# Attention in double steps with shift groups of two pairs, a reordered beginning, and later turns of the feed-forward inputs

## The reference

```
x = x + attention(layernorm(x))     # 16 heads of 64; q, k, v, softmax over 256, heads (with swapped axes) @ Wp + bp
x = x + ffn(layernorm(x))           # layernorm with gain and bias, w1 (512 x 128) and w2 (128 x 512) rounded to
                                    # -1, 0, 1 by their mean size, exact gelu, a second layernorm over 512
```

## Time and profile before

| what | value |
|---|---|
| median of 3 runs | 992.97 us (990.68 to 994.6) |
| profiled execution, its own time | 992.29 us |
| its span, first to last instruction | 990.5 us |
| granted TensorE clock, mean of the core | 1.000 |
| busy share PE / DVE / ACT / POOL | 98 / 86 / 74 / 87% |

### The profile page before, as it was taken

How to read it: one execution, slowest core, us unless ns; L and a number is a source line. 1 busy time by engine, 2 the same in 40 slices (tenths; PEclk the granted TensorE clock), 3 DMA queues, 4 the chain that set the end, 5 groups by cost and what they waited for, 6 DMA issues and landing times.

```text
span 990.5 us, 39211 instructions
## 1 busy us (share of the span) xinstructions
PE 968.2 (98%) x15932; PEld 767.8 (78%) x15932; DVE 854.4 (86%) x1743; ACT 733.4 (74%) x1180; POOL 861.8 (87%) x849
## 2 busy tenths in 40 slices
PE   7899999999999999999999999999999999989998
PEld 6577777787787887777778878877888887767776
DVE  6898988888888898899888988898888988768787
ACT  4687777778777777777777777777777778677775
POOL 5789898989886999999999999999899999878885
PEclk9999999999999999999999999999999999999999
DMA  6112232342323333223333332233433333367885
GB/s 136 44 31 53 47 74 53 62 64 64 79 43 51 64 84 65 61 51 59 85 63 64 58 83 39 61 61 83 65 63 64 63 64 63 79 126 158 168 171 129
DMA packets 242786, 74.08 MB, mean 75 GB/s; under 512 B 218032, under 2 KB 240304, under 8 KB 242608
## 3 DMA queue, kind: packets, MB, share of 16 engines
q1 hardware_dynamic: 240528, 71.05, 36.7%
q10 hardware_dynamic: 2080, 0.52, 0.3%
HBM read 11.41 MB, written 8.39 MB: 20 GB/s over the span
## 4 chain that ended last, share of the span: by engine, by line
PE 92%; DVE 2%; ACT 2%; issue 1%; DMA 1%; POOL 1%; SPq 0%; DVEq 0%; ACTq 0%; POOLq 0%
PE S L765 11%; PE PV L790 8%; PE M L725 7%; PE PV L792 6%; PE PV L791 6%; PE QK L712 5%; PE QK L714 5%; PE QK L713 5%; PE misc L765 5%; PE S L757 5%; PE M L843 2%; PE M L808 2%; PE M L845 2%; PE M L844 2%; PE misc L757 2%; PE M L810 2%
## 5 line engine op out<-in xcount | busy, mean ns | idle before, releaser
L1325 POOL TENSOR_TENSOR pl<-p 128x1024 f16<-128x1024 f32 x253 | 476.6, 1896 | 33.1 <-ACT p L1102 32.8
L1526 DVE TENSOR_REDUCE negmax<-M 128x4 f32<-128x1024 f32 x252 | 306.7, 1217 | 22.2 <-PE M L725 16.2
L1110 ACT ACTIVATE QKh<-QK 128x512 f16<-128x512 f32 x251 | 149.5, 596 | 142.2 <-PE QK L714 141.4
L1102 ACT ACTIVATE p<-S,s_exp 128x1024 f32<-128x1024 f32 x173 | 192.2, 1111 | 56.9 <-PE S L765 56.3
L790 PEld LDWEIGHTS PV<-V,p 128*128 128x128 bf16 x2048 | 186.6, 98 | 47.1 <-issue 36.3
L790 PE MATMUL PV<-V,p 128*128 128x65 f16 x2048 | 214.8, 193 | 4.5 <-DVE O L1540 3.6
L791 PE MATMUL PV<-V,p 128*128 128x64 f16 x2048 | 213.2, 192 | 0.0
L792 PE MATMUL PV<-V,pl 128*128 128x65 f16 x2048 | 212.5, 194 | 0.0
L1546 DVE TENSOR_TENSOR QKl<-QK,QKh 128x512 f16<-128x512 f32 x251 | 172.3, 687 | 43.3 <-ACT QKh L1110 42.2
L791 PEld LDWEIGHTS PV<-V,p 128*128 128x128 bf16 x2048 | 189.0, 97 | 4.7
L792 PEld LDWEIGHTS PV<-V,pl 128*128 128x128 f16 x2048 | 188.7, 97 | 0.0
(11 more groups left out here) (246 smaller groups left out, 2472.4 us busy)
## 6 DMA issues: line engine op xcount, KB each, us to landing
y_kept<-yTb SPq DMA_DIRECT2D x32, 128.0 KB, 1.7
yT<-y_kept SPq DMA_DIRECT2D x16, 256.0 KB, 3.4
result<-X SPq DMA_DIRECT2D x15, 256.0 KB, 3.0
X<-in_L_attn_query SPq DMA_DIRECT2D x7, 512.0 KB, 4.2
OT<-O SPq DMA_TRANSPOSE x64, 4.1
shift<-negmax SPq DMA_TRANSPOSE x63, 2.3
O<-in_L_attn_Wk ACTq DMA_DIRECT2D x2, 256.0 KB, 4.8
O<-in_L_attn_Wq SPq DMA_DIRECT2D x2, 256.0 KB, 5.6
```

The lines of the kernel that those rows point to most:

```text
L1102: e.activation(p32[r][:, :, :, :].rearrange("p i m n -> p (i m n)"), score_bank(p)[:, :], ACT.Exp, scale=s_exp[:, :]).then_inc(s_ex, 1)
L1325: e.tensor_tensor(pl[r][:, :, :, :].rearrange("p i m n -> p (i m n)"), p32[r][:, :, :, :].rearrange("p i m n -> p (i m n)"), p_high(r).rea ...
L1526: e.tensor_reduce(dst[:, :, NB * jj:NB * jj + NB], max_bank(p)[:, :].rearrange("p (i t m) -> p i t m", i=2, t=NB), AX.X, ALU.max, negate=T ...
```

## The change

It does eight things:

1. GP is 2 instead of 4: 128 shift groups instead of 64. Q_LEAD goes from 7 to 5, MAX_LEAD from 6 to 4. `shift_in` becomes two semaphores, one for each buffer.
2. Ahead of step 0 stand now pairs 0 to 3 of queries and keys and 0 to 2 of maxima. On ACT, the part up to step 0's end is written out in a new order; Wv's scaling comes ahead of the first shift, Wvh behind exps(0).
3. The statistics of batch 2 go from step 0 to 4, its norm, split and bias follow later too. The maxima of Wp and g2 go from ahead of step 0 to step 9, and P_SCALED and P_LOW behind them.
4. TWO_0 is 56 instead of 80: 24 more pairs run in double steps.
5. As MEAN2 and BIAS2 now fall into double steps, their products go to the upper half of M behind the projection, and the next double step waits for DVE's result of them (`PREPARED`). ACT, POOL and DVE call `weights` in double steps.
6. Steps of the weights move: GAINS2 59 to 58, MEAN2 64 to 62, T2_SPLIT 66 to 64, BIAS2 72 to 66.
7. Y_TURN goes from 6 to 8 and Y_KEEP from 8 to 12.
8. At the end PAIRED is NP - 4 instead of NP - 6, and DVE makes two low halves of p instead of three.

```
-GP = 4
+GP = 2
-Q_LEAD, MAX_LEAD, PV_LAG = 7, 6, 3
+Q_LEAD, MAX_LEAD, PV_LAG = 5, 4, 3
-Y_LAG, Y_LOW, Y_TURN, Y_KEEP = 2, 4, 6, 8
+Y_LAG, Y_LOW, Y_TURN, Y_KEEP = 2, 4, 8, 12
-PAIRED = NP - 6
-TWO_0, TWO_1 = 80, 240
-LOW_ON_DVE = (NP - 5, NP - 3, NP - 1)
+PAIRED = NP - 4
+TWO_0, TWO_1 = 56, 240
+LOW_ON_DVE = (NP - 3, NP - 1)
-MAXIMA = {"pg": (None, 7, 8), "t1": (45, 46, 54)}
+MAXIMA = {"pg": (9, 10, 11), "t1": (45, 46, 54)}
-T1_SPLIT, GAINS2, MEAN2, T2_SPLIT, BIAS2 = MAXIMA["t1"][2] + 1, 59, 64, 66, 72
+T1_SPLIT, GAINS2, MEAN2, T2_SPLIT, BIAS2 = MAXIMA["t1"][2] + 1, 58, 62, 64, 66
+PREPARED = {MEAN2: "T2_less", BIAS2: "bias2"}
...
 def qk_pairs(t):
-    first = {0: [5, 6], 1: [7, 8], 2: [9], TWO_1: []}
+    first = {0: [4, 5], TWO_1: []}
...
 def max_pairs(t):
-    first = {0: ([], [5]), 1: ([6], [7])}
+    first = {1: ([4], [5])}
+    if t == 0:
+        return [3], []
...
-    return b + 2 if j == (2 if in_two(HP * b) else 0) and 1 <= b + 2 < B else None
+    return b + 2 if j == (2 if in_two(HP * b) else 0 if b else 4) and 1 <= b + 2 < B else None
...
             def scores(p):
-                    e.wait_ge(shift_in, 16 * g)
+                    e.wait_ge(shift_in[g % 2], shift_turned(g))
...
                 if p == TWO_0 + 1:
                     e.wait_ge(s_x1, TWO_0 // HP - 2)
+                    e.wait_ge(s_w, W_AT["clip_t1"])
...
             def two_steps(t):                       # PE
                 if t > TWO_0:
                     e.wait_ge(*two_free(t - 2))
+                    if t - 2 in PREPARED:
+                        e.wait_ge(s_w, W_AT[PREPARED[t - 2]])
...
                 if two_project(t):
                     project_tile(*two_project(t), t)
+                second_weights(t)
                 weighted(t - 1)
...
+            def second_weights(t):
+                dst = M[:, 512:1024]
+                if t in PREPARED:
+                    e.wait_ge(s_mx, t + MAX_LEAD + 2)
                 if t == MEAN2:
...
             maxima_spread("v")
+            max_scores(2)
             queries_keys(3)
-            max_scores(2)
-            e.wait_ge(s_mx, 2)
-            kept_busy(3)
-            max_scores(3)
-            queries_keys(4)
             first_shift_turned()
-            max_scores(4)
...
             w_high(1)                               # ACT
             qk_high(0)
+            w_high(2)
             qk_high(1)
             qk_high(2)
-            w_high(2)
-            qk_high(3)
-            x_high(1)
-            qk_high(4)
             w_high(3)
-            first_shift()
             e.wait_ge(s_w, W_AT["inv_v"])
             e.activation(Wv, Wv, ACT.Identity, scale=inv[:, 2:3]).then_inc(s_hi, 1)
+            first_shift()
+            qk_high(3)
+            exps(0)
+            qk_high(4)
             e.wait_ge(s_hi, HI_AT["Wv_scaled"])
             e.activation(Wvh[:, :], Wv, ACT.Copy).then_inc(s_hi, 1)
+            qk_high(5)
+            shift_rounded(1)
+            x_high(1)
...
-            for p in range(2, FIRST):               # DVE
-                qk_low(p)
-            e.wait_ge(p_in, P_IN)
-            largest_of(3, t2_rows(Wp), "part_p")
-            e.wait_ge(ffn_in, FFN_IN)
-            largest_of(4, g2[:, :], "part_g")
+            qk_low(2)
+            qk_low(3)
```

More of the change, by code:

```diff
@@ L106, in x_stats_batch @@
 def x_stats_batch(b, j):
-    return b + 2 if j == (2 if in_two(HP * b) else 0) and 1 <= b + 2 < B else None
+    return b + 2 if j == (2 if in_two(HP * b) else 0 if b else 4) and 1 <= b + 2 < B else None
 def x_norm_tile(b, j):
-    return (b + 2, j - 1) if j in (1, 2) and 2 <= b + 2 < B else None
+    first = 1 if b else 5
+    return (b + 2, j - first) if j in (first, first + 1) and 2 <= b + 2 < B else None
 def x_split_batch(b, j):
-    return b + 2 if j == (5 if in_two(HP * b) else 3) and 1 <= b + 2 < B else None
+    return b + 2 if j == (5 if in_two(HP * b) else 3 if b else 7) and 1 <= b + 2 < B else None
 def x_bias_batch(b, j):
-    return b + 2 if j == (7 if in_two(HP * b) else 5) and 1 <= b + 2 < B else None
+    return b + 2 if j == (7 if in_two(HP * b) or b == 0 else 5) and 1 <= b + 2 < B else None
 def two_values(t):
@@ L234, in misc_uses @@
             yield "bias1", 0
[L235 to L238, removed]
 def value_order():
@@ L296, in qk_bank_before @@
 def qk_bank_before(p):
-    first = {0: None, 1: None, 2: None, 3: 0, 4: 1, 5: 3, 6: 4, 7: 5, 8: 6, 9: 7, 10: 9}
+    first = {0: None, 1: None, 2: None, 3: 0, 4: 1, 5: 3, 6: 5}
     return first.get(p, p - 1)
@@ L402, in layer @@
         ot_in = [sem(f"s_outputs_transposed{c}") for c in range(H // HH)]
-        xt_in, shift_in = sem("s_x_transposed"), sem("s_shift_transposed")
+        xt_in = sem("s_x_transposed")
+        shift_in = [sem(f"s_shift_transposed{i}") for i in range(2)]
         yt_in, y_kept_in = sem("s_ffn_y_transposed"), sem("s_ffn_y_kept")
@@ L453, in misc_done @@
                     "tern": lambda: (s_w, W_AT[f"cmp{key}"]), "last": lambda: (s_w, W_AT["T1_last"]),
-                    "bias1": lambda: (s_w, W_AT["bias1"]), "mean2": lambda: (s_w, W_AT["T2_less"]),
-                    "bias2": lambda: (s_w, W_AT["bias2"])}[kind]()
+                    "bias1": lambda: (s_w, W_AT["bias1"])}[kind]()
         last_out = misc_banks[0][:, 0:D]
@@ L467, in qk_bank @@
                 return misc_banks[misc_bank_no("qk", 2)]
-            return PV if p in (1, 4, 6, 8) else QK
+            return PV if p in (1, 4) else QK
         def max_bank(p):
-            return S if p in (1, 3) else M
+            return S if p == 1 else M
         def score_bank(p):
@@ L487, in two_free, with shift_turned @@
             return (s_x0, first_tiles(b)) if tile == 0 else (s_x1, b + 1)
+        def shift_turned(g):
+            return 16 * ((g + 1) // 2)
         def head_rows(i):
@@ L645, in sp_program @@
                         turn_shift(shift_group(t))
+                    if t == 0:
+                        turn_x(1)
                     if x_split_batch(*divmod(t - 1, HP)) is not None:
@@ L782, in weighted @@
                 else:
-                    e.wait_ge(s_qklo, 9)
+                    e.wait_ge(s_qklo, 5)
                 for t in range(NB):
@@ L1088, in shift_rounded @@
                 if g >= 3:
-                    e.wait_ge(shift_in, 16 * (g - 2))
+                    e.wait_ge(shift_in[g % 2], shift_turned(g - 2))
                 elif g == 1:
@@ L1202, in two_steps @@
                 qk_high(t + Q_LEAD + 2)
+                weights(t)
+                weights(t + 1)
             def y_norm(b):
@@ L1434, in pool_program @@
             w_low(2)
-            x_low(1)
             w_low(3)
-            add_bp(0)
             e.wait_ge(s_hi, HI_AT["Wv"])
             e.tensor_tensor(Wvl[:, :], Wv, Wvh[:, :], ALU.subtract).then_inc(s_lo, 1)
+            x_low(1)
+            add_bp(0)
             add_bp(1)
@@ L1588, in weights @@
             def weights(t):
+                if t == MAXIMA["pg"][0]:
+                    e.wait_ge(p_in, P_IN)
+                    largest_of(3, t2_rows(Wp), "part_p")
+                    e.wait_ge(ffn_in, FFN_IN)
+                    largest_of(4, g2[:, :], "part_g")
                 if t == SUMS:
@@ L1696, in two_steps @@
                     residual_tile(*two_project(t))
+                weights_held(t)
                 sums_inverse(t - 1)
```

15 lines of the change are left out of this document (6 added, 9 removed).

## The result

The changed kernel takes 995.85 us, median of 11 runs (994.76 to 996.52), against 992.35 us, median of 11 runs of the kernel before on the same chip. The ratio is 1.0035, with a 95% interval of 1.0026 to 1.0044: slower by 0.35%. Forecast were 990.2 us, so the forecast missed by 5.7 us: the time is just inside the upper edge of the range (985.5 to 996), but on the other side of the kernel before.

The account below looks back on a forecast made before the run. PE, busy 98% of the span, was taken as the bound, with DVE leading the start. Terms -3.2 + 0.4 + 0 + 0 = -2.8 us from 992.29 give 989.5, or 990.2 us on the median's scale; range 985.5 to 996.

Parts of the forecast that it names:

- the last sentence on the shift groups: SP's queue: moving yTb's turn from lag 6 to 8 keeps it off the shift and delays no y_norm; cost 0.
- The end, 0 plus or minus 1: Last pairs: shift group, maximum and PAIRED move together, with PE's longest wait there, 1.86 us, keeping its causes; 0 us.
- The start: Before the first weighted sum: DVE leads and gets less work; 5.5 us gross, 3.5 net of put-off PE work, -3.2 finally.
- the four items' 5.5 us: DVE before the first weighted sum: two maxima 2.3, two QKl 1.2, maxima of Wp and g2 1.3, batch 2 statistics 0.7.
- The absorption: Early steps: DVE's moved 2.0 us (Wp and g2, statistics) fit its free time, at a cost of 0.3 us.
- rival A: The start gives -6 us and ACT hides GAINS2, so double steps give -0.7; near 986.3 us; chance 0.25.
- Double steps from 56: Pairs 56 to 80 as double steps: 84.75 us against 84.29, +0.4 us, bounds -1.5 and +2.
- change of kind: Switch from single to double steps: costs 2.3 us, moves to step 55, where T1's scaling and split may add 0.2.
- Rival D: Double steps from 56 stall several us on new waits of MEAN2, BIAS2 or clip_t1; 995 at most; no separate chance given.
- Twice the shift groups: 64 more ACT roundings and SP turning DMAs, hidden in slack; 0 us, up to +1.8.
- Rival B: The rounding at j = 4 on ACT does not fit: 0.08 us in each of 23 batches, 992.0 us; chance 0.13.
- Rival C: At j = 0 the shift lands late behind OT, PE waits once per batch; 1013 us at one us each; chance 0.10.

Follow-up runs that it names:

- run 1: The kernel after with yTb's turn back at lag 6 and its keeping at 8: 992.32 us, ratio to the kernel before 0.9994.
- run 3: The kernel after with yTb's turn at lag 6 and its keeping left at 12: 992.07 us, ratio to the kernel before 0.9987.
- run 5: The kernel after with yTb's turn and keeping at lags 6 and 8 from batch 28 on, 8 and 12 before: 989.62 us, ratio 0.9964.
- run 10: The kernel before with only the maxima of Wp and g2 moved to step 9: 993.67 us, ratio 1.0008.
- run 11: The kernel of run 5 with the maxima of Wp and g2 back ahead of step 0: 988.97 us, ratio 0.9966.
- run 7: The kernel after with one extra unread rounding on ACT at j = 4 of each double step: 996.39 us, ratio 1.0035.
- run 8: The kernel after with four extra unread roundings on ACT at j = 4 of each double step: 1002.07 us, one execution.
- run 9: The kernel after with double steps from 80 and GAINS2, MEAN2, T2_SPLIT, BIAS2 24 steps later: 996.89 us, ratio 1.005.
- run 6: The kernel after with yTb's turn issued ahead of the turned output at step 256: 993.34 us, ratio 1.0004.
- run 4: The kernel after with 40 identity transposes on PE ahead of its wait for the fourth gelu: 994.6 us, ratio 1.0021.
- run 12: The kernel of run 5 with the sums of w1 and w2 split over steps 17 and 18: 988.74 us, ratio 0.9964.

## Why the prediction missed, step by step

**The step that failed** is the last sentence on the shift groups: that the yTb turn goes to the other side of the shift "keeps that turn's issue out of its way; y_norm, which waits for that turn, comes at the end of j = 2, over 5 us later ... Cost 0". The first half is right, and worth more than I gave it: runs 1 and 3 show three late shifts each without it, some 3.1 us. "Over 5 us later" is right in double steps. At the end it isn't: the queue's order changes there (`turned_halves` takes the step itself and not two steps before), SP waits 7.7 us for the data of the OT ahead, and later the turns of zT lie between. I read the queue in steady state and used it for every batch. Measured: +6.0 us from exponential 255 to the end, +0.5 with the lag put back in the last batches (run 5). "The end, 0 plus or minus 1" is right for what it looked at: the wait of the earlier trace rows is still 1.86 us.

**The start** was forecast at -3.2: -5.5 gross, +2.0 put off, +0.3 absorbed. scores(0) came at 21.19 us (20.62 in run 5; forecast 20.6), the first weighted sum at 32.63 (31.68 in run 1, 32.06 in run 5; forecast 31.8). The profiled execution of the kernel after had a low clock early on (below); from the first projection to the first weighted sum it takes 18.55 us, to the hundredth what run 1 takes, and the 0.95 us between them lie ahead of the first projection. Before, that stretch took 24.25 us. So the gross size is right: 5.7 us by this measure, 5.6 us in run 1 from the span's start. Its make-up is not: run 10 shows that, in the kernel before, 1.3 of the four items' 5.5 us lay in DVE's wait for PE and were not on the path. That the sum came out all the same is luck; what made up for the 1.3 us (perhaps what the shorter lead saves on the loop of PE, ACT and DVE) was not tried. The hand-followed figure hid this. The absorption was sized at 0.3 and is 1.1 us (run 1 is 5.59 us ahead at the first weighted sum and 4.48 at exponential 24); 0.7 to 0.8 of it are the maxima of Wp and g2 (runs 10 and 11). The put-off work came back at the end as said: 1.75 us against 2.0, exponential 248 to 255. Net the start gave 1.8 us in the kernel after (3.54 - 1.75) and 2.7 in run 1 (4.48 - 1.75), against 3.2, so rival A, with 6, falls.

**Double steps from 56**: +0.4 forecast, -0.39 measured, within the bounds. The three batches from 56 take 299.40 - 218.11 = 81.29 us, 2.24 over 79.05, and the starts of the exponentials say where. GAINS2 was sized about right: 58 to 60 takes 8.30 us in place of 7.13 and 60 to 62 takes 5.90 in place of 6.15, 0.9 us against 1.1. MEAN2 and BIAS2 add 2.0 us, against 2.1. The mis-sized term is the change of kind with T1's split: 2.61 us more from 48 to 56, as forecast (2.5), but 56 to 58 then takes 5.95 us in place of 6.64, so it is 1.9 us in all. The wait near steps 58 to 60 that the prediction asked for is there, in two parts, behind GAINS2 on ACT:

```profile
229.87 1.27 ACT L1160 ACTIVATE above<-tern,gs 128x128 f32<-128x128 f32 x4
...
235.73 0.28 PE L717 MATMUL QK<-xT,Wh 128*128 128x256 f16 x1 [0.51 <-DVE QKl L1562]
236.93 0.39 PE L730 MATMUL M<-QKh 64*128 64x256 f16 x4 [0.37 <-DVE V L1568]
```

The rows name DVE, but DVE had come late from ACT, which runs without a gap from 229.37 us to the exponentials of step 62: the first part grows to 0.61 us with one rounding more on ACT (run 7) and to 0.89 with four (run 8), and in run 9, with GAINS2 at step 82, the same two waits (0.50 and 0.37 us) stand at 314.5 and 315.7 us. Run 9's 0.87 us agrees with the terms' 0.8, but it is two things: 24 plain pairs take 80.4 us in single steps (6.70 us for two pairs in run 9) and 79.05 in double steps, 1.3 us less, and about 0.4 of it go to a dearer change of kind at 56. No step waits for the new semaphores; one more wait of PE, 0.95 us ahead of exponential 56, is for a low half on POOL. Rival D falls, and that the measured time lies near its 995 us is chance.

**Twice the shift groups**: 0 forecast, 0 measured, 26.35 us per batch. Rival B falls, for more room than I thought (runs 7 and 8). Rival C, the wait for a shift, occurs in the double steps only with the yTb turn ahead of it, and then now and then (run 1: 2 of 23 batches), not in each batch. The rule weighed in the prediction (the Trainium skill, "DMA: Bandwidth & Descriptors", Rules for kernel authors) gave an estimate of +128 us for the 64 small turns, had they been exposed; the trace of the kernel after has them hidden to the last one. The 2 us in that estimate are the same page's figure (the Trainium skill, "DMA: Bandwidth & Descriptors", Anatomy of one DMA) for DMAs that GpSimd issues; these go out from SP, and land in 2.3 us (median of 127).

## What to carry to other kernels

An in-order queue that issues DMAs must be read at each place where the order of the steps changes, its last batches above all: name the instruction ahead of the moved one there, and what that one waits for. A constant that shifts work by two steps everywhere can be right in the middle and wrong at the end; a second value for the last batches is cheap. And busy time before a wait is not path: see whether the engine waits for another one right behind the work taken away, for then the work was free.

## What the runs showed that was not expected

- PE's granted clock early in the span differs between executions, with the same instructions ahead: the kernel after had 0.57 on average from 10 to 14 us, in runs 1 and 6 it was 1.00 there. The first weighted sum is 0.95 us later with it (32.63 against 31.68 in run 1). It is so in all profiles with this beginning: 31.2 to 31.7 us in the five with 1.00 (runs 1, 4, 6, 7, 9), 32.1 to 32.6 in the five with 0.57 to 0.70 (the kernel after, runs 3, 5, 8, 12). What decides it was not found.

```profile
10.00:14.00 4.00, 4.00 (x23) 3.71 (x22) 3.00 (x9) 2.34 (x5) 0.00 (x0) 0.57 0.82 223
```

- Transposes of the identity alone, 40 in 4.53 us, left the clock at 1.00 (run 4), where a wait of 4.86 us was followed by 0.50. The Trainium skill, "TensorE: Matmul & The Clock Gate", Part 4 (PE-mode transpose), has it that the full clock doesn't engage for transposes; in this trace it was held through them, so the trace does not agree in so far. Whether they would raise it from 0.50 was not run.
- The turn of a shift tile (32 KB) takes 2.3 us in the median and 4.2 us behind two other turns in the queue (run 1). That is enough to make 2 in 23 late in the double steps, at a place where the prediction saw 1.9 us to spare.
